# Rotary attention and expert layer on one core: the cosine product moved into PSUM, weight splits moved, unread TensorE products added

## The reference

```python
# layer 1: attention, H = 16 heads of D = 128
q = rope(einsum('bim,mhd->bhid', ln(x), wq)); k = rope(einsum('bim,mhd->bhid', ln(x), wk))
v = einsum('bim,mhd->bhid', ln(x), wv)
s = (q / 128**.5) @ (k / 128**.5).T - 1e30 * (i < j)
x = x + ln(einsum('bhid,hdm->bim', softmax(s) @ v, wo))
# rope: even * cos - odd * sin | even * sin + odd * cos  (halves of D)
# layer 2: 16 experts of width 256, the best 4 for each token
logits = ln(x) @ router_weight.T + router_bias ; top 4, softmax over them
out_e = ((clip(up) + 1) * gate * sigmoid(1.702 * gate)) @ down_e + bias_e
x = x + ln(sum over the 4 chosen e of score_e * out_e)
```

## Time and profile before

| | us |
|---|---|
| median of three runs | 542.02 |
| the profiled execution | 541.4 |
| its span, first to last instruction | 539.6 |
| TensorE busy with products | 458.9 (85%) |
| VectorE busy | 356.9 (66%) |
| ScalarE busy | 326.6 (61%) |
| GpSimd busy | 250.4 (46%) |

### The profile page before, as it was taken

How to read it: one execution, slowest core, us unless ns; L and a number is a source line. 1 busy time by engine, 2 the same in 40 slices (tenths; PEclk the granted TensorE clock), 3 DMA queues, 4 the chain that set the end, 5 groups by cost and what they waited for, 6 DMA issues and landing times.

```text
span 539.6 us, 11513 instructions
## 1 busy us (share of the span) xinstructions
PE 458.9 (85%) x3388; PEld 430.5 (80%) x3388; DVE 356.9 (66%) x1231; ACT 326.6 (61%) x810; POOL 250.4 (46%) x229
## 2 busy tenths in 40 slices
PE   2888889999999999999999998334999999999700
PEld 2787778899999999999999997324999999999600
DVE  3799777778676677766685854251776776766436
ACT  3677777677587677676767666132566565655402
POOL 1778675536222256344552253141355555555612
PEclk9999999999999999999999999755999999999955
DMA  7336652699800001001464567023366656655482
GB/s 228 103 118 204 204 178 87 205 371 368 282 2 21 1 13 44 23 24 56 142 213 143 154 213 224 1 83 109 52 101 104 98 94 102 105 88 91 52 235 94
DMA packets 63900, 67.86 MB, mean 126 GB/s; under 512 B 4640, under 2 KB 58720, under 8 KB 63840
## 3 DMA queue, kind: packets, MB, share of 16 engines
q1 hardware_dynamic: 54960, 55.79, 32.5%
q0 software_dynamic: 8304, 10.88, 12.2%
q10 hardware_dynamic: 576, 0.46, 0.3%
HBM read 32.63 MB, written 34.49 MB: 124 GB/s over the span
## 4 chain that ended last, share of the span: by engine, by line
PE 66%; DVE 16%; issue 6%; ACT 4%; DMA 3%; POOL 3%; SPq 1%; DVEq 0%; POOLq 0%; ACTq 0%
PE bank L1087 25%; PE bank L1313 16%; PE bank L1325 7%; PE bank L1146 4%; PE bank L1128 4%; DVE qkT L818 3%; PE bank L1136 2%; DVE by_cos L809 2%; PE bank L1300 2%; PE bank L1127 2%; PE bank L1148 2%; DVE stats L789 1%; ACT by_sin L565 1%; POOL rows_d L458 1%; DVE oT_l L843 1%
## 5 line engine op out<-in xcount | busy, mean ns | idle before, releaser
L455 POOL TENSOR_TENSOR by_sin<-by_sin,rope_sin 128x512 f32<-128x512 f32 x64 | 83.0, 1297 | 150.9 <-ACT by_sin L565 150.9
L555 POOL DMA_INDIRECT sum_d<-y,xg x47 | 73.1, 1555 | 74.7 <-ACT y L753 74.4
L1313 PE MATMUL bank<-xgT,gu_now 128*128 128x128 f32 x752 | 93.3, 278 | 0.4 <-DVE gu_now L1024 0.4
L565 ACT ACTIVATE by_sin<-bank 64x512 f32<-64x512 f32 x128 | 75.8, 592 | 24.2 <-DVE by_cos L809 22.7
L1313 PEld LDWEIGHTS bank<-xgT,gu_now 128*128 128x128 f32 x752 | 89.4, 195 | 0.7 <-DVE gu_now L1024 0.7
L1087 PE MATMUL bank<-xT_h,qk_h 128*128 128x256 f32 x256 | 78.6, 307 | 3.5 <-POOL qk_l L440 2.0
L1087 PE MATMUL bank<-xT_h,qk_l 128*128 128x256 f32 x256 | 73.5, 287 | 0.0
L1087 PE MATMUL bank<-xT_l,qk_h 128*128 128x256 f32 x256 | 73.2, 286 | 0.0
L587 ACT ACTIVATE prob<-score,row_bias 128x128 f32<-128x128 f32 (+1 forms) x128 | 56.9, 447 | 22.4 <-DVE row_bias L828 22.1
L843 DVE TENSOR_TENSOR oT_l<-bank,oT_h 128x256 fp32r<-128x256 f32 x64 | 27.1, 423 | 59.2 <-ACT oT_h L565 56.8
L818 DVE TENSOR_TENSOR qkT<-by_cos,by_sin 128x512 f32<-128x512 f32 x64 | 55.6, 869 | 1.1 <-POOL by_sin L455 1.1
(11 more groups left out here) (140 smaller groups left out, 1131.8 us busy)
## 6 DMA issues: line engine op xcount, KB each, us to landing
rows_d<-blank SPq DMA_DIRECT2D x32, 576.0 KB, 7.2
gu_w<-_L_ffn_gate_up_proj_dram SPq DMA_DIRECT2D x16, 512.0 KB
xg<-rows_d SPq DMA_DIRECT2D x47, 144.0 KB
dn_w<-in_L_ffn_down_proj_dram SPq DMA_DIRECT2D x16, 256.0 KB
sum_d<-blank SPq DMA_DIRECT2D x2, 1152.0 KB, 9.8
raw_qk<-in_L_attn_wq_dram SPq DMA_DIRECT2D x16, 128.0 KB, 3.5
raw_qk<-in_L_attn_wk_dram SPq DMA_DIRECT2D x16, 128.0 KB, 3.7
raw_v<-in_L_attn_wv_dram SPq DMA_DIRECT2D x8, 256.0 KB, 2.8
```

What stands on the lines that cost most here:

```text
L455: pool.tensor_tensor(v, v, rope_sin[:, :].unsqueeze(1).broadcast_to([P, 2, T]), ALU.mult).then_inc(pool_sin, 1)
L555: pool.indirect_dma_start(out=sum_d[i % SUMS], out_offset=bass.IndirectOffsetOnAxis(ap=xg[:, i % XG, TOKEN:TOKEN + 1].bitcast(U32), axis=0 ...
L565: return sc.activation(out, in_, ACT.Copy)
L1313: m = pe.matmul(ps_gu[i % 2][:, (2 * s + r) * P:(2 * s + r + 1) * P], gu_now[:, i % 2, k, s, r * P:(r + 1) * P], xgT[:, i % XT, k, :], sta ...
```

## The change

The tile `by_cos` is gone. `swap(n)` now waits for `qk_chunk(n)` alone; `cosine(n)` waits for `swap(n)` and multiplies in place in the PSUM bank; `rotate(n)` reads that bank and `by_sin`. The bank is free for `qk_chunk(n+2)` when `rotate(n)` is done. `cosine(n+4)` goes behind `normalise_prob(n+1)` in VectorE's slot. In the first batch the split of head 5 is done ahead of the slots, `high_qk` of the later heads at the end of the slot before, and `high_v` one slot earlier, in the even slots. TensorE gets products whose results nobody reads: 4 of 512 columns at the start (on a tile that VectorE clears first), 48 of 128 columns after the attention, then 2, 4 and 2 of 256 columns between the steps of the routing and 22 after the table.

```diff
-        by_cos = part("by_cos", [P, 2, 2 * T])
@@ gpsimd
             low_qk(4)
+            low_qk(5)
             times_sine(3)
@@
-                if b == 0 and h + 5 < H:
+                if b == 0 and h >= 1 and h + 5 < H:
                     low_qk(h + 5)
@@ scalar
             def swap(n):
-                sc.wait_ge(dve_cos, n + 1)
+                sc.wait_ge(pe_qk, n + 1)
@@
             swap(3)
+            high_qk(5)
             softmax_exp(0)
             for n in range(SLOTS):
                 b, h = n // H, n % H
-                if b == 0 and h + 5 < H:
-                    high_qk(h + 5)
@@
                 if b == 0:
-                    if h % 2 == 1 and h // 2 + 2 < H // 2:
+                    if h + 6 < H:
+                        high_qk(h + 6)
+                    if h % 2 == 0 and h // 2 + 2 < H // 2:
                         high_v(h // 2 + 2)
@@ vector
             def cosine(n):
-                dve.wait_ge(pe_qk, n + 1)
-                if n >= 2:
-                    dve.wait_ge(dve_rope, n - 1)
-                v = by_cos[:, n % 2, :].rearrange("p (b t) -> p b t", b=2)
-                dve.tensor_tensor(v, ps_qk[n % 2][:, :].rearrange("p (b t) -> p b t", b=2),
-                                  rope_cos[:, :].unsqueeze(1).broadcast_to([P, 2, T]), ALU.mult).then_inc(dve_cos, 1)
+
+                dve.wait_ge(act_swap, n + 1)
+                v = ps_qk[n % 2][:, :].rearrange("p (b t) -> p b t", b=2)
+                dve.tensor_tensor(v, v, rope_cos[:, :].unsqueeze(1).broadcast_to([P, 2, T]), ALU.mult).then_inc(dve_cos, 1)
@@
-                dve.tensor_tensor(qkT[:, n % QR, :, :].rearrange("p w t -> p (w t)"), by_cos[:, n % 2, :], by_sin[:, n % 2, :],
+                dve.tensor_tensor(qkT[:, n % QR, :, :].rearrange("p w t -> p (w t)"), ps_qk[n % 2][:, :], by_sin[:, n % 2, :],
                                   ALU.add).then_inc(dve_rope, 1)
@@
+            dve.memset(qkT[:, 0, :, :], 0.0).then_inc(dve_idle, 1)
             dve.wait_ge(dma_x[0], 16)
@@
             rotate(0)
-            cosine(2)
+            rotate(1)
             dve.wait_ge(dma_mask, 16)
             row_max(0)
-            rotate(1)
+            cosine(2)
+            rotate(2)
             cosine(3)
-            rotate(2)
             normalise_prob(0)
@@
                     rotate(n + 3)
+                if n + 1 < SLOTS:
+                    normalise_prob(n + 1)
                 if n + LEAD < SLOTS:
                     cosine(n + LEAD)
-                if n + 1 < SLOTS:
-                    normalise_prob(n + 1)
@@ tensor, qk_chunk
                 if n >= 2:
-                    pe.wait_ge(act_swap, n - 1)
+                    pe.wait_ge(dve_rope, n - 1)
@@ router_logits
                 if r == B - 1:
-                    pe.wait_ge(act_swap, SLOTS)
+                    pe.wait_ge(dve_rope, SLOTS)
@@
+            def keep_busy(lhs, rhs, count, out=bank[4]):
+
+                for _ in range(count):
+                    pe.matmul(out[:, 0:rhs.shape[-1]], lhs, rhs, start=True, stop=True)
+
+            pe.wait_ge(dve_idle, 1)
+            keep_busy(qkT[:, 0, 0, 0:P], qkT[:, 0, :, :].rearrange("p w t -> p (w t)"), 4)
@@ after output_rows(SLOTS - 1)
+            spare = up_to[:, :, :].rearrange("p a b -> p (a b)")
+            for c in range(48):
+                pe.matmul(bank[4][:, 0:P], wo_h[:, c % H, 0:P], xT_h[:, 1, 0, 0:P], start=True, stop=True)
             turn_moe(B - 1)
+            keep_busy(ident[:, :], spare, 2)
             router_logits(B - 1)
+            keep_busy(ident[:, :], spare, 4)
             ranks(B - 1)
             counts()
             turn_route(B - 1)
             start_sums(B - 1)
+            keep_busy(ident[:, :], spare, 2)
             pe.wait_ge(dve_plan, 1)
@@
             m.then_inc(pe_table, 1)
+            keep_busy(ident[:, :], spare, 22, bank[7])
```

More of the change, by code:

```diff
@@ L238, in block_kernel @@
         dve_stat = sem("dve_stat")
+        dve_idle = sem("dve_idle")
         dve_var = sem("dve_var")
```

## The result

The changed kernel takes 545.81 us (median of 4 runs, 544.83 to 546.10) where the kernel before takes 541.92 (median of 4, 540.69 to 542.04): the ratio is 1.0076, 95% interval 1.0063 to 1.0089. It is slower by 3.9 us, and I had forecast 540.6, a slight gain that could hardly be told from nothing (the terms of the sum make 540.5). The range, 534.5 to 546.5, holds the result near its upper end; the likeliest case, with its own range up to 543.8, does not. The profiled execution took 545.94, span 544.1, against 541.4 and 539.6.

The account below looks back on a forecast made before the run. Attention was taken as TensorE-bound from the second batch, with 12.7 us to be had in the first. Profile: 541.4 - 1.8 - 2.2 + 5.8 + 0.2 - 3.5 = 539.9; plus 0.6 for the median, 540.5, rounded 540.6; range 534.5 to 546.5.

Parts of the forecast that it names:

- stall at `high_v`: First batch: ScalarE asks for the value weights before their load lands, losing 0.7 to 1 us in slots 6, 8, 10.
- part 3: Batches two to four: slots with statistics, residual or token placing delay TensorE, 1.95 us per batch, a loss of 5.8 us.
- the ring: Attention slots: chain of swap, cosine, row maxima, exponentials, probability copy and next swap, about 3.9 us, fitting a plain 4.50 slot.
- part 4: Last heads of attention: row maxima of head 61 come 1.2 us later, ScalarE hides 1.0, a loss of 0.2 us.
- part 1: First batch without its head: fifteen slots take 79.4 us against 81.2, a gain of 1.8 us, ends 0 and 6.
- part 2: Head of the program: four early products raise TensorE's clock, a gain of 2.2 us, ends -1 and 3.
- part 5: Passage from attention to expert tiles: unread products keep TensorE's clock up, a gain of 3.5 us, ends -3 and 5.
- kept at 2.4: Passage ahead of the first tile: at 2.4 GHz transposes, logits and ranks shorten, a gain of 1.6 us.
- A: First batch: GpSimd's multiply starts late enough for the cast to slip in, 5.0 us a slot, 536.2 us; chance 0.20.
- B: Passage: the 48 products last over 0.135 us each and delay the transposes; at 0.22, 544.7 us; chance 0.20.
- D: Head: the four products leave the clock down, 2.7 us less gained, 543.2 us; chance 0.05.
- C: Attention slots: swap-to-swap chain exceeds 4.50 us, cosine into PSUM costing 0.6 more; at 4.6, 545.4 us or more; chance 0.10.

Follow-up runs that it names:

- Experiments 1: Changed kernel with the cosine one slot later, behind row maxima and `oT_low`, right ahead of its add: 530.93 us, ratio 0.9794.
- Experiment 2: Changed kernel with the rotary part undone (`by_cos` back in SBUF, cosine ahead of the swap), moved splits and unread products kept: 539.97 us, ratio 0.9965.
- experiment 5: Changed kernel with `high_v` alone moved back to the odd slots: 541.87 us, ratio 1.0004.
- Experiment 4: Changed kernel without the 2, 4 and 2 unread products between the routing steps, the 48 and 22 kept: 544.84 us, ratio 1.0068.
- Experiment 9: Kernel before with all the unread products of the change, rotary part and weight splits as before: 538.76 us, ratio 0.9946.
- experiment 8: Changed kernel without the cleared tile and the four 512-column products at the start: 546.86 us, ratio 1.0101.
- experiment 6: Changed kernel with the first batch's cast `high_o` moved ahead of the cosine: 540.48 us, ratio 0.9978.
- Experiment 7: Changed kernel with `high_o` ahead of the cosine and `high_v` back in the odd slots: 535.28 us, ratio 0.9879.
- experiment 3: Changed kernel without the 48, 2, 4, 2 and 22 unread products between attention and tiles: 547.91 us, ratio 1.0113.
- 11: Changed kernel with the cosine a slot later, `high_v` back in odd slots, and no 2, 4 and 2 products: 529.76 us, ratio 0.979.

## Why the prediction was wrong

The sum said -1.5 us from profile to profile; it was +4.5. The 6.0 between them: 3.9 at head 15 (a gain of 4.0 forecast, of 0.05 measured), of which 3.4 is the first batch behind its head and 0.5 the head; 1.65 in the passage; and 0.4 in the final sums. The 3.4 are what the third stall at `high_v` cost in this trace beyond an ordinary landing.

**The later batches (part 3) were right.** Forecast 5.8. Measured: 6.0 from head 15 to 63. The output products of head 18 were put at 129.0 and started at 128.86, their wait at 1.5 and it was 1.20. By slots, slot 1 adds 0.3 already and slot 2 1.2, slot 7 about 0.5. Experiments 1 and 2 show the cause from two sides: moving the cosine out of the ring, or taking the ring out, brings 226.6 and 226.3 us against 226.3 before. Slots 3 to 5 carry the delay along, as said. The 0.2 for the last heads (part 4) did not come: heads 61 to 63 keep their spacing. This is why the change is slow: in a batch bound by TensorE it had nothing to gain and a reserve to lose.

**The first batch (part 1) had its mechanisms right and one size wrong.** Forecast was a gain of 1.8 for the fifteen slots (79.4 us), measured a loss of 1.6 (82.84).
- The step that failed is the stall at `high_v`, put at 0.7 to 1 us in slots 6, 8 and 10, some 2.5 in all, from a landing of 2.8 us and with no term for TensorE's clock. The slots are right, and with `high_v` back the fifteen slots take 77.62 us (experiment 5): it costs 5.2 in the changed kernel's trace, 2.7 more than put down. ScalarE waited 0.54, 1.17 and 3.36. In the third, the load was issued 3.6 us after the swap ended (79.67 to 83.28), 0.3 more than the step's 3.3; it landed in 4.4 and not in 2.8, the median; and ScalarE asked 4.7 us after that swap and not 5.4. With the 0.7 of the step, these 0.3, 1.6 and 0.7 make 3.3. Then the clock fell to half for 3.4 us, which no step had. Experiment 4 has the same first batch with a landing of 2.6 and no such fall, and there that slot is 1.86 us shorter and the one behind it 1.57: without these 3.4 the fifteen slots of the changed kernel would take the 79.4 forecast. Experiment 2 shows the stall without the ring.
- The row quoted for the landing gives 4.8 as its maximum, but that is the very first load of the program; in the slots the kernel before had 2.5 to 3.4, so its trace gave no sign of this. Over the thirteen traces the last of the eight loads took 4.2 to 5.2 us in seven and 2.6 to 3.1 in six, the kernel before among these. Why is open. In its old slot `high_v` is not held up by it (5.2 us in experiment 5).
- That the rest comes to 79.4 is in part luck. All sixteen casts were blocked, 0.59 each (0.871 less 0.286), for which the prediction itself had 81 us; 79.4 stood between all and none. In slots 1 and 3 a small tensor_scalar of the statistics was blocked too, 1.16 and 1.15 us where the kernel before had 0.63 and 0.47, of which I had not thought. On the other side the slots without a stall take 77.62 (experiment 5) and not 81 - 2.5 = 78.5, and the stalls with an ordinary landing make 79.4 - 77.6 = 1.8 and not 2.5. The Trainium skill (SBUF — State Buffer, SBUF: two separate sides) says that a GpSimd operation and a VectorE one in a two-port mode, or with two SBUF inputs, exclude each other for the whole instruction. The trace agrees: the add, with one input in PSUM, never exceeds 0.692, while the cast, SBUF to SBUF, takes 0.76 us at least where it meets the multiply.

**The head (part 2)** was close: 1.7 at head 0's output products against 2.2, and it was right to add it to the total. Experiment 9, the kernel before with the products, keeps its 1.5 us from head 0 to head 15, and experiment 8 keeps 1.7 to head 10, where the clock's fall in the changed kernel's trace hides it. In the changed kernel the lead over the kernel before falls from 1.7 at head 0 to 0.3 at head 1 (37.56 against 37.86), but this belongs to part 1: from head 0 to 1 it takes 6.81 us against 5.45, and with the cast ahead of the cosine 5.05 (experiment 6).

**The passage (part 5)** was forecast at 3.5 and gave 1.85 in this profile. Its cost was right: the 48 products took 5.47 us (0.114 each; 5.3 forecast, and not the 3.9 that stands beside it there) and the 22 ended ahead of tile 0. Of its gains, the first tile's gate and up products run at full clock, and that came; but "kept at 2.4" failed for the 1.6 us ahead of tile 0. The clock fell at 353.3 although TensorE had paused only 1.2 us since the 48 products. Six other traces with the same products (experiments 1, 2, 5, 6, 8 and 9) have their fall some 14 to 15 us behind attention, past the logits; there the term is 3.3 to 3.6, as forecast. Experiment 7, with its first fall at 344.6, 6.5 us behind attention as in the changed kernel, again has 29.85 us to tile 0. By the medians the products of the passage gave the changed kernel 2.1 (experiment 3). So the size hangs on where the fall lies. There is one trace of each kernel, and what sets the place is open.

**The rivals.** A (the cast slips in) is out for this order: 16 of 16 blocked; but experiments 1 and 6 show that a change of order makes it true. B is out by 0.114 a product, D by the spacing of 0.12 at the head. C is out: the cosine in place costs 0.700 against 0.685, and the plain slots keep their length (heads 23 to 31: 38.08 us against 38.06). The Trainium skill's remark (ScalarE: Activation LUTs, Step-by-step: what each stage is for) that VectorE is closer to SBUF is quoted in the prediction for this; the difference measured here is 0.015 us. The slower side came true by a cause that was inside my own forecast and not among the rivals. The stall should have been a case of its own, with a slow landing and a fall of the clock as its price, and the ends of part 1 (a gain of 0 to 6) should have reached to a loss.

## What to carry to other kernels

A wait that is harmless on average sits in an in-order queue: when an operation is moved behind another engine's, list what stands behind it in the slots that carry extra work, and place it last in its slot, right ahead of its consumer (the cosine one slot later brought the end of attention 13.4 us forward, of which some 1.6 is the clock's fall in the changed kernel's trace). When a step that needs a load is moved forward, ask what it costs if one landing is 1.5 us late and TensorE's clock falls behind it, and not only what the median landing costs. A gain at the head can be checked head by head: here it was carried on, and the one number at head 15 hid that. And before a difference between two traces is put down to an edit, look at how far traces of the same code differ: here up to 3 us at head 15, by one landing and one fall of the clock.

## What was unexpected of the hardware

- A pause of TensorE of 2.2 us in the first batch (86.9 to 89.15) was followed by 3.4 us at half clock from 90.5; in experiment 8 the same pause, 2.23 us at the same place, was not. In the passage, pauses of 1.2 us behind 5.47 us of dense products were followed in the changed kernel and experiment 7 by a fall 6.5 us behind attention, in six other traces by one only past the logits. In all of them the clock came back after 3.4 us, where without the products it was down for 30.7 us (before) and 34.1 (experiment 3), and without the 2, 4 and 2 for 13.7 (experiments 4 and 11).
- The same 256 KB load, the last of its kind in the first batch, lands in 2.6 to 3.1 us in six traces and in 4.2 to 5.2 in seven.
- Products of 128 columns in fp32r run at 0.114 us each, hardly faster than those of 256 (0.12 apart).
- An operation of two elements on VectorE is held up by a whole GpSimd instruction: 1.16 us against 0.17 (in the kernel before too, 1.15 at 120.35).
- A VectorE product in place in PSUM costs 0.700 us, the same product from PSUM into SBUF 0.685.
